# A three-stage graph pipeline on one core: one semaphore per step, packed float32 scores, a new order of work

## The chip, the cores and the metric

The kernel runs on one NeuronCore of a Trainium2 chip. A core has a matrix engine (TensorE, PE in the rows), a vector engine (VectorE, DVE), a scalar engine for activation functions (ScalarE, ACT), GpSimd (POOL) and SyncE (SP), which here only issues DMAs. Each engine runs its own list of instructions strictly in order, and the engines meet through semaphores: an instruction waits until a counter has reached a value, and raises another when it is done. The metric is the time of one execution on the device in microseconds, as the median of several.

## What is computed

Sixteen graphs of 512 nodes with 256 features each go through four layers, each on the layer-normed and rectified state, each added to the state:

```python
h = relu(layernorm(x)); x = x + L0(h, adj)   # hypergraph convolution twice, layer norm between them, plus h
h = relu(layernorm(x)); x = x + L1(h, adj)   # attention "transition" matrix, two hops
h = relu(layernorm(x)); x = x + L2(h, adj)   # 8 heads of 32 features
h = relu(layernorm(x)); x = x + L3(h, adj)   # relu((adj @ h) @ K) * mask

# L1: e = leaky_relu(sj[j] + si[i] + ab);  alpha = A * exp(e);  T = alpha / rowsum(alpha)
#     H = X W0 + T X W1 + T T X W2 + biases, then relu
# L2: Xp = X Wp (per head), Xc = Xp C^T;  attn = tanh(A * (Xc Xp^T));  out = relu(attn Xp)
```

## The kernel before

One graph is four tiles of 128 nodes (NT = 4) by 256 features. The work is a software pipeline over graphs. Every engine has a list of steps that it goes through once for each turn; a step is written with a delay, and in turn b it works on graph b minus that delay. Steps whose names begin with `f_` are the front, layers L0 and L1; steps whose names begin with `k_` are the back, layers L2 and L3. In each turn PE does the front of one graph and the back of the graph before it, so that the matmuls of the back fall where the front waits for a hand-off. The loop body is written out once and run by a hardware loop; the first and last turns are unrolled. A graph's back ends one turn after its front, so the last graph's back runs alone.

The front, in order, with the matmuls of each step: `f_m` and `f_u` (incidence transposed times h, incidence times that), `f_conv1` (times W1), `f_zT` (transposes of the normed hidden state z), `f_xw` (times W2), `f_m2`, `f_y` (incidence products again), `f_hT` (transposes of L1's input h1), `f_sj` and `f_q` (products of h1 with weights), then the softmax-like part on ACT and DVE (`f_exp`: two exponentials for each of four row tiles; `f_alpha`: their maximum and the product with adj; `f_sums`, `f_trans`: the division), `f_tt` (transposes of the transition matrix), `f_r` and `f_x2` (the two hops). Nearly every product is made in split float32: each operand is a high part and a low part of type fp32r, and three products (`three`) stand in for one. For this each PSUM tile is read twice: ACT copies it out as the high part, and DVE then subtracts that copy from the PSUM tile and writes the low part. Such a pair is called a hand-off below. PSUM holds three one-bank tiles `ring_f` for the front, two two-bank tiles `ring_b` for the back, and one bank `pv_acc` in which the attention output is summed.

The back: `k_norm2`, `k_hT`, `k_xp`, `k_xc` (projections of all heads), then eight attention units `k_unit` 0 to 7. A unit is four heads by one tile of 128 rows: PE makes the scores of four heads (`k_scores`), DVE multiplies them by the adjacency tile (the gate, L972, two halves of 1024 columns), ACT takes tanh (L579, two halves), and PE multiplies the result with Xp (`k_attend`, L1292, four matmuls into four strips of 32 columns). Then `k_outT`, layer norm 3 (`k_stats3`, `k_norm3`), `k_ax` (adjacency times h, plain float32) and `k_out`.

The scores are made by stacking: three 32-row groups (high, high, low of one operand against high, low, high of the other) are put on 96 partitions of `stk_p` and `stk_c`, by 24 DMAs a graph issued on SP (L331), after DVE and POOL have made the high and low parts (L952, L447, L956). One fp32r matmul of 96 rows then does a head's scores. `ring_b` has two halves, and the scores of a unit's second half can start as soon as DVE has read that half.

DMA loads are issued on SP in the order x, adjT (`rows`), the weight row (`wrow`), adj, adjT again for the back (`at`), and the store. `next_x` waits for `xh_sum` (POOL has read the x before), `next_adjt` for the transposes of `f_tt`. POOL computes the reciprocal roots of the layer norms with a power (L409, L413).

Every engine has one or two counting semaphores for most of its outputs (`drained`, `hi_made`, `full`, `full_b`), which are raised in the order of the code. A step that is moved therefore changes the counts of all.

## Time and profile before

| what | value |
|---|---|
| runs of the kernel before | 1858.55 us median of 3 (1858.37 to 1859.98) |
| profiled execution: device time, span | 1858.6 us, 1856.8 us |
| PE busy | 1544.6 us, 83% |
| DVE busy | 1193.9 us, 64% |
| ACT busy | 892.4 us, 48% |
| POOL busy | 273.9 us, 15% |
| mean granted TensorE clock | 0.92 |

The profiled execution's time is 1.8 us above its span, and 0.05 us above the median. A row of the timeline gives start, duration, engine, line, operation, output and inputs, shapes, and in brackets how long the engine was idle before it and who released it. Matmuls are pipelined: the next group starts before the duration of the last one has run out, so lengths of PE work are read as differences of starts. A float32 matmul appears as two records.

### The profile page before, as it was taken

How to read it: one execution, taken by the hardware profiler on the slowest of the kernel's cores; microseconds unless marked ns; L12 is line 12 of the kernel's file. 1: busy time of each engine (PE TensorE's matmuls, PEld its weight loads, DVE VectorE, ACT ScalarE, POOL GpSimd, SP SyncE). 2: the span in 40 equal slices, each digit the busy share in tenths (PEclk: the TensorE clock that was granted, in tenths of full speed). 3: DMA queues.
4: the chain of work that ended last, by engine and by line, in shares of the span. 5: the costliest groups of instructions: out<-in, count | busy, mean ns of one | idle time of the engine just before them, and what ended most of it. 6: DMA issues, size and time to landing. Idle time of an engine off the chain costs nothing.

```text
span 1856.8 us, 26984 instructions
## 1 busy us (share of the span) xinstructions
PE 1544.6 (83%) x9334; PEld 1195.9 (64%) x9334; DVE 1193.9 (64%) x2650; ACT 892.4 (48%) x1479; POOL 273.9 (15%) x167
## 2 busy tenths in 40 slices
PE   5587988989889888988989898897989889888855
PEld 4576675757667576776757677675767667666632
DVE  5565758677575866757585675758667575765523
ACT  2335546454454645445454534645454464545433
POOL 1101120111202011120201112020111201112010
PEclk8788998989899898989989898998989999898978
DMA  5013132132313213231321323123031412313030
GB/s 157 12 52 79 52 99 67 35 80 74 90 51 93 71 34 79 73 90 51 82 82 34 79 73 90 51 69 94 23 90 57 107 51 58 85 44 80 22 81 11
DMA packets 80806, 125.51 MB, mean 68 GB/s; under 512 B 10177, under 2 KB 29185, under 8 KB 80769
## 3 DMA queue, kind: packets, MB, share of 16 engines
q1 hardware_dynamic: 80768, 125.02, 24.1%
q8 instruction: 23, 0.38, 0.1%
q14 instruction: 15, 0.11, 0.0%
HBM read 66.27 MB, written 8.39 MB: 40 GB/s over the span
## 4 chain that ended last, share of the span: by engine, by line
PE 51%; DVE 16%; issue 16%; ACT 10%; POOL 6%; SPq 1%; DMA 0%; DVEq 0%; POOLq 0%; ACTq 0%
PE ring_f L1026 29%; PE ring_b L1026 15%; DVE att L972 7%; ACT hf L488 3%; PE ring_f L1182 2%; POOL xp_s L447 2%; POOL xf L430 2%; POOL xf L428 2%; ACT att L601 1%; PE ring_f L1212 1%; DVE rows L904 1%; PE ring_f L1124 1%; PE pv_acc L1292 1%; DVE rows L885 1%; POOL rstd_f L409 1%
## 5 line engine op out<-in xcount | busy, mean ns | idle before, releaser
L1026 PE MATMUL ring_f<-m,inc_n 128*128 128x256 f32 x2048 | 324.6, 289 | 16.7 <-POOL m L420 14.1
L972 DVE TENSOR_TENSOR att<-ring_b,at 128x1024 f32<-128x1024 f32 x256 | 299.2, 1216 | 35.7 <-PE ring_b L1026 33.8
L579 ACT ACTIVATE att<-att 128x1024 f32<-128x1024 f32 x256 | 263.6, 1066 | 100.3 <-DVE att L972 94.3
L1026 PEld LDWEIGHTS ring_f<-m,inc_n 128*128 128x128 f32 x2048 | 289.8, 194 | 25.1 <-issue 20.8
L1026 PE MATMUL ring_b<-stk_c,stk_p 96*128 96x512 f32 x512 | 186.8, 483 | 61.5 <-DMA stk_c<-xc_s 44.5
L1026 PE MATMUL ring_f<-m,inc_t 128*128 128x256 f32 x1024 | 210.3, 284 | 14.5 <-DVE m L742 14.5
L1026 PE MATMUL ring_f<-w,uz 128*128 128x256 f32 (+1 forms) x896 | 188.9, 334 | 13.1 <-DVE uz L735 8.5
L1026 PEld LDWEIGHTS ring_b<-stk_c,stk_p 96*128 96x128 f32 x512 | 100.2, 223 | 148.0 <-issue 71.4
L409 POOL TENSOR_TENSOR rstd_f<-var_f,mhalf 128x4 f32<-128x4 f32 x48 | 48.5, 1010 | 922.2 <-DVE var_f L726 922.2
L1026 PEld LDWEIGHTS ring_f<-w,uz 128*128 128x128 f32 x896 | 152.3, 192 | 34.2 <-DVE uz L735 14.9
L1026 PEld LDWEIGHTS ring_f<-m,inc_t 128*128 128x128 f32 x1024 | 160.3, 191 | 17.7 <-DVE m L742 17.7
L1292 PE MATMUL pv_acc<-att,xp_n 128*32 128x512 f32 x1024 | 134.2, 607 | 30.9 <-ACT att L579 29.9
L481 ACT ACTIVATE m<-ring_f,be 128x256 fp32r<-128x256 f32 x128 | 53.7, 470 | 170.9 <-PE ring_f L1026 169.0
L1026 PE MATMUL ring_b<-at,hb 128*128 128x512 f32 x256 | 117.8, 605 | 7.4 <-ACT hb L589 7.4
L474 ACT ACTIVATE uz<-ring_f 128x512 fp32r<-128x512 f32 x128 | 73.2, 598 | 100.2 <-PE ring_f L1124 43.0
L742 DVE SCALAR_TENSOR_TENSOR m<-ring_f,be,m 128x256 fp32r<-128x256 f32 x128 | 56.0, 479 | 83.0 <-ACT m L481 81.7
L1026 PE MATMUL ring_b<-xc_s,wp 128*128 128x512 f32 x192 | 72.9, 553 | 42.1 <-ACT att L601 38.8
L1026 PE MATMUL ring_f<-wk,uz 128*128 128x256 f32 x768 | 104.5, 285 | 0.0
L735 DVE TENSOR_TENSOR m<-ring_f,uz 128x512 fp32r<-128x512 f32 x64 | 41.4, 686 | 95.6 <-ACT uz L474 95.6
L1026 PEld LDWEIGHTS ring_f<-wk,uz 128*128 128x128 f32 x768 | 97.4, 191 | 2.8 <-DVE inc_t L735 2.7
L735 DVE TENSOR_TENSOR m<-ring_f,m 128x512 fp32r<-128x512 f32 x64 | 43.9, 687 | 85.7 <-ACT m L474 85.7
L488 ACT ACTIVATE hf<-xf,off_f,rstd_f 128x256 f32<-128x256 f32 x64 | 33.2, 589 | 136.8 <-DVE off_f L730 136.8
(158 smaller groups left out, 2623.7 us busy)
## 6 DMA issues: line engine op xcount, KB each, us to landing
stk_p<-xp_s SPq DMA_DIRECT2D x192, 128.0 KB, 2.4
stk_c<-xc_s SPq DMA_DIRECT2D x192, 128.0 KB, 2.3
rows<-in_adjT SPq DMA_DIRECT2D x16, 1024.0 KB, 5.3
adj_n<-in_adj SPq DMA_DIRECT2D x16, 1024.0 KB, 8.5
at<-in_adjT SPq DMA_DIRECT2D x16, 1024.0 KB, 5.3
x_in<-in_x SPq DMA_DIRECT2D x16, 512.0 KB, 3.5
out_x<-xb SPq DMA_DIRECT2D x16, 512.0 KB, 2.9
wrow<-in_adj SPq DMA_DIRECT2D x16, 256.0 KB, 6.0
```

The costliest lines, as they stand in the source:

```text
L409: pool.tensor_tensor(rstd_f[:, k], var_f[:, k], mhalf[:], ALU.pow).then_inc(rstd_made.sem, 1)
L428: pool.tensor_tensor(xf[:], x_in[:], hf[:], ALU.add).then_inc(xh_sum.sem, 1)
L430: pool.tensor_tensor(xf[:], xf[:], b2_bc[:].unsqueeze(1).broadcast_to([P, NT, D]), ALU.add).then_inc(xh_sum.sem, 1)
L474: act.activation(dst, ring_f[tile % 3][:], ACT.Copy).then_inc(hi_made.sem, 1)
L481: ins = act.activation(dst_of(t), ring_f[tile % 3][:, i * D:(i + 1) * D], ACT.Copy, scale=be[:, t:t + 1])
L488: ins = act.activation(dst[:, i], src[:, i], ACT.Relu, bias=off[:, i:i + 1], scale=scale[:, i:i + 1])
L579: act.activation(v, v, ACT.Tanh).then_inc(tanh_made.sem, 1)
L735: dve.tensor_tensor(dst, ring_f[tile % 3][:], hi_part.bitcast(F32), ALU.subtract)\
L742: ins = dve.scalar_tensor_tensor(dst_of(t), ring_f[tile % 3][:, i * D:(i + 1) * D], be[:, t:t + 1], hi_of(t).bitcast(F32), ALU.mult, ALU.s ...
L972: dve.tensor_tensor(att[:, u % 2, 2 * half:2 * half + 2], pair(tile)[:], at[:, t].unsqueeze(1).broadcast_to([P, 2, N]), ALU.mult)\
L1026: ins = pe.matmul(dst, lhsT, rhs, start=(first and n == 0), stop=(last and n == len(pairs) - 1), skip_group_check=True)
L1292: ins = pe.matmul(pv_acc[h * KH:(h + 1) * KH, :], xp_n[:, t, ch:ch + KH], att[:, u % 2, h], start=(t == 0), stop=(t == NT - 1), skip_group ...
```

## The change

- Every step has a semaphore of its own. The bank that a front tile uses comes from a table (`TILES`, `BANKS`).
- No stacking: `xp_t` and `xc_t` hold Xp and Xc as float32 with the four heads of a part on four groups of 32 partitions. The scores of a unit are four float32 matmuls with 32 rows each, one after another, into the four banks of `ring_b`. The 24 DMAs a graph, the high and low parts of Xp (DVE L952, POOL L447) and the low part of Xc (DVE L956) go. All four banks are written at once, so a unit's scores wait until both halves of the unit before it have been gated.
- L1's `si` comes from two more columns of `wq` (258 columns in `f_q`), with one small DVE addition for each row tile; the four DVE products of `f_si` (L868) go. `f_exp` for row tile i now waits for `f_q` i. The copy of the state `k_keep` (L941) goes: `f_x2` writes to `xa`, and `k_outT` writes `xb` from it.
- The high and low parts of the transposed transition matrix are in `tr_h` and `tr_l`, no longer in `inc_n` and `inc_t`.
- The turn is cut at another place (`f_m` is the first step of PE's list), and the steps are in another order on all engines. Attention units run from `f_zT` on: on PE scores 0 stands ahead of `f_xw`, scores 1 behind it. On SP the load of x stands behind that of adjT, the store and `wrow`.

The core of the diff (the steps' bodies mostly only change the names of their semaphores). The lists of steps at its end are the orders of a turn on SyncE, TensorE, ScalarE and VectorE, in this sequence; the number ahead of a step is its delay:

```diff
-            def stack(dst, src, part, group, loaded):
-
-                for h in range(4):
-                    sp.dma_start(
-                        dst[32 * group:32 * group + 32, h:HEADS:4, :].bitcast(F32),
-                        src[32 * h:32 * h + 32, part, :].rearrange("p (t n) -> p t n", t=2).bitcast(F32),
-                    ).then_inc(loaded.sem, 16)
...
             def k_scores(g, u):
                 part, t = divmod(u, NT)
                 if u == 0:
-                    pe.wait_ge(stk_p_loaded.sem, stk_p_loaded.after(g, STACK_LOADS))
-                    pe.wait_ge(stk_c_loaded.sem, stk_c_loaded.after(g, STACK_LOADS))
-                for half in range(2):
-                    ps = bank_b(g, B_S + 2 * u + half)
-                    for k in range(2):
-                        h = 4 * part + 2 * half + k
-                        ins = products(ps[:, k], [(stk_p[0:STACK, h, t * P:(t + 1) * P], stk_c[0:STACK, h])])
-                    ins.then_inc(full_b.sem, 1)
+                    pe.wait_ge(xc_made.sem, xc_made.after(g, 1))
+                    pe.wait_ge(xn_made.sem, xn_made.after(g, 1))
+                else:
+                    pe.wait_ge(gated.sem, gated.after(g, 2 * u))
+                for h in range(4):
+                    head = slice(h * KH, (h + 1) * KH)
+                    ins = pe.matmul(ring_b[h // 2][:, h % 2], xp_t[head, part, t * P:(t + 1) * P], xc_t[head, part],
+                                    start=True, stop=True, skip_group_check=True)
+                    if h % 2 == 1:
+                        ins.then_inc(scored.sem, 1)
...
              def f_exp(g, i):
-
                 if i == 0:
-                    act.wait_ge(si_made.sem, si_made.after(g, 2))
-                    act.wait_ge(full.sem, full.after(g, T_SJ + 1))
+                    act.wait_ge(sj_full.sem, sj_full.after(g, 1))
+                act.wait_ge(si_made.sem, si_made.after(g, i + 1))
...
             # SyncE, the order of a turn
-                    (-1, next_x), (-1, next_adjt), (-1, next_wrow), (-1, next_adj), (0, next_at), (1, store),
-                    (0, stack_p), (0, stack_c),
+                    (0, next_adjt), (3, store), (0, next_wrow), (0, next_x), (0, next_adj), (1, next_at),
...
             # TensorE, the order of a turn
-                    (0, f_u), (0, f_conv1), (1, k_hT), (2, k_out), (1, k_xp), (0, f_zT), (0, f_xw, 0), (0, f_xw, 1),
-                    (1, k_xc), (0, f_m2), (0, f_y), (1, k_scores, 0), (0, f_hT), (1, k_scores, 1), (0, f_sj),
-                    (0, f_q, 0), (1, k_attend, 0), (1, k_scores, 2), (1, k_attend, 1), (1, k_scores, 3),
-                    (1, k_attend, 2), (1, k_scores, 4), (0, f_q, 1), (0, f_q, 2), (1, k_attend, 3), (0, f_q, 3),
-                    (1, k_scores, 5), (1, k_attend, 4), (0, f_tt), (0, f_r, 0), (1, k_scores, 6), (1, k_attend, 5),
-                    (1, k_scores, 7), (0, f_r, 1), (1, k_attend, 6), (1, k_attend, 7), (1, k_outT), (0, f_x2, 0),
-                    (0, f_x2, 1), (1, k_ax, 0), (-1, f_m), (1, k_ax, 1),
+                    (0, f_m), (2, k_out), (0, f_u), (1, k_hT), (0, f_conv1), (1, k_xp), (1, k_xn), (1, k_xc),
+                    (0, f_zT), (1, k_scores, 0), (0, f_xw, 0), (0, f_xw, 1), (1, k_scores, 1), (0, f_m2),
+                    (1, k_attend, 0), (1, k_scores, 2), (0, f_y), (1, k_scores, 3), (1, k_attend, 1),
+                    (1, k_attend, 2), (1, k_scores, 4), (1, k_attend, 3), (0, f_hT), (1, k_scores, 5), (0, f_sj),
+                    (0, f_q, 0), (1, k_attend, 4), (0, f_q, 1), (1, k_scores, 6), (0, f_q, 2), (0, f_q, 3),
+                    (1, k_attend, 5), (1, k_scores, 7), (1, k_attend, 6), (0, f_tt), (0, f_r, 0), (1, k_attend, 7),
+                    (0, f_r, 1), (1, k_outT), (0, f_x2, 0), (0, f_x2, 1), (1, k_ax, 0), (1, k_ax, 1),
...
             # ScalarE, the order of a turn (after)
+                    (0, f_h0), (2, k_xh, 1), (1, f_r, 0), (1, f_r, 1), (2, k_h3), (2, k_ax), (0, f_m), (1, k_h2),
+                    (0, f_u), (1, k_hT), (2, k_out), (0, f_relu), (1, k_xp), (0, f_z), (1, k_xn), (1, k_xc),
+                    (0, f_zT), (0, f_xw, 0), (0, f_xw, 1), (1, k_unit, 0), (0, f_m2), (1, k_unit, 1),
+                    (1, k_unit, 2), (1, k_unit, 3), (0, f_h1), (0, f_hT), (1, k_xh, 0), (1, k_unit, 4),
+                    (0, f_q, 0), (0, f_q, 1), (0, f_exp, 0), (0, f_q, 2), (0, f_q, 3), (0, f_exp, 1),
+                    (0, f_exp, 2), (0, f_exp, 3), (1, k_unit, 5), (1, k_unit, 6), (0, f_tt), (1, k_unit, 7),
...
             # VectorE, the order of a turn (after)
+                    (0, f_stats0), (0, offset, 0), (0, f_HT), (0, f_h0), (1, f_r, 0), (1, f_r, 1), (2, k_outT),
+                    (2, k_stats3), (2, offset, 4), (0, f_H), (2, k_mask), (1, f_x2, 0), (0, f_dn), (1, f_x2, 1),
+                    (1, k_stats2), (2, k_ax), (0, f_m), (1, offset, 3), (0, f_u), (1, k_hT), (0, f_conv1),
+                    (0, offset, 1), (0, f_zT), (1, k_unit, 0), (0, f_xw, 0), (0, f_xw, 1), (1, k_unit, 1),
+                    (0, f_m2), (1, k_unit, 2), (0, f_y), (0, f_stats2), (1, k_unit, 3), (0, offset, 2),
+                    (1, k_unit, 4), (0, f_hT), (1, k_unit, 5), (0, f_q, 0), (0, f_q, 1), (1, k_unit, 6),
+                    (0, f_alpha, 0), (0, f_q, 2), (0, f_q, 3), (0, f_alpha, 1), (0, f_alpha, 2), (0, f_alpha, 3),
+                    (0, f_sums), (0, f_trans), (0, f_tt), (1, k_unit, 7),
```

What stands in a row on SP in the loop body, of the kernel before (a row is one DMA instruction, what it waits for in brackets; ISA rows are waits):

```order
L284 ISA [waits xh_sum]
L284 DMA x_in<-in_x 128x4x256
L374 ISA
L293 ISA [waits full]
L293 DMA rows<-in_adjT 128x4x512
L364 ISA
L290 DMA wrow<-in_adj 128x512 [waits drained]
L369 ISA
L287 DMA adj_n<-in_adj 128x4x512 [waits trans_made]
```

And of the changed kernel, the start of SP's loop body:

```order
L324 ISA [waits tt_full]
L324 DMA rows<-in_adjT 128x4x512
L394 REGISTER_ALU
L395 ISA [waits y_made]
L395 DMA out_x<-xb 128x4x256
L321 DMA wrow<-in_adj 128x512 [waits dn_read]
L362 ISA
L315 ISA [waits xh_sum]
L315 DMA x_in<-in_x 128x4x256
L318 DMA adj_n<-in_adj 128x4x512 [waits trans_made,dn_read,incn_made]
```

The load of x was the first of the turn, with a wait of its own. Now it stands behind the wait for the transposes of `f_tt` (`tt_full`), and behind the issues of adjT, of the store and of `wrow`.

ACT around the place where the next graph's first activation and the copy of the attention output stand (hf<-x_in is `f_h0` of the next graph, xh_t<-pv_acc the copy that PE's `k_outT` waits for, m<-ring_f the high parts of `f_r`, hb<-xb layer norm 3), before:

```order
L474 ACTIVATE m<-ring_f 128x512 [waits full]
L473 REGISTER_ALU
L474 ACTIVATE m<-ring_f 128x512 [waits full]
L606 REGISTER_ALU
L488 ACTIVATE hf<-x_in,off_f,rstd_f 128x256 [waits off_made]
L488 ACTIVATE hf<-x_in,off_f,rstd_f 128x256 x3
L573 ACTIVATE xh_t<-pv_acc 128x512 [waits pv_made]
L589 ACTIVATE hb,msum<-xb,off_b,rstd_b 128x256 [waits off_b_made]
```

And after:

```order
L469 ISA [waits off_made0]
L471 REGISTER_ALU [waits xh_sum]
L462 ACTIVATE hf<-x_in,off,rstd 128x256 [waits max_made]
L462 ACTIVATE hf<-x_in,off,rstd 128x256 x3
L594 ISA
L452 ACTIVATE xh_t<-pv_acc 128x512 [waits pv_made]
L452 ACTIVATE m<-ring_f 128x512 [waits r_full] x2
L598 REGISTER_ALU
L600 REGISTER_ALU [waits off_made4]
L602 ACTIVATE hb,msum<-xb,off,rstd 128x256 [waits mask_made]
```

`f_h0` now stands ahead of the high parts of `f_r`, and still ahead of the copy xh_t; both belong to the turn that is ending.

ACT in the softmax part, after the change (m<-ring_f is the high part of a `f_q` tile, the pairs rows<-ring_f and hf<-ring_f are the two exponentials of one row tile, att<-att is tanh of half a unit, here of units 5 and 6):

```order
L452 ACTIVATE m<-ring_f 128x256 [waits q_full] x2
L539 ACTIVATE rows<-ring_f,si 128x512 [waits si_made,sj_full]
L542 ACTIVATE hf<-ring_f,si 128x512
L452 ACTIVATE m<-ring_f 128x256 [waits q_full] x2
L539 ACTIVATE rows<-ring_f,si 128x512 [waits si_made]
L542 ACTIVATE hf<-ring_f,si 128x512
L539 ACTIVATE rows<-ring_f,si 128x512 [waits si_made]
L542 ACTIVATE hf<-ring_f,si 128x512 [waits max_made]
L539 ACTIVATE rows<-ring_f,si 128x512 [waits si_made]
L542 ACTIVATE hf<-ring_f,si 128x512 [waits max_made]
L586 REGISTER_ALU
L588 ACTIVATE att<-att 128x1024 [waits gated]
```

And PE at the same place (wq products are `f_q` 2 and 3; pv_acc<-att is `k_attend` 5 and 6, ring_b<-xc_t is `k_scores` 7, ident,rows is `f_tt`):

```order
L992 MATMUL ring_f<-wq,uz 128x258 [waits q_lo,h1_lo]
L992 MATMUL ring_f<-wq,uz 128x258 x5
L992 MATMUL ring_f<-wq,uz 128x258 [waits q_lo,h1_lo]
L992 MATMUL ring_f<-wq,uz 128x258 x5
L1267 MATMUL pv_acc<-att,xp_n 32x512 [waits tanh_made]
L1267 MATMUL pv_acc<-att,xp_n 32x512 x3
L1248 REGISTER_ALU
L1251 MATMUL ring_b<-xc_t,xp_t 128x512 [waits gated]
L1251 MATMUL ring_b<-xc_t,xp_t 128x512 x3
L1267 MATMUL pv_acc<-att,xp_n 32x512 [waits tanh_made]
L1267 MATMUL pv_acc<-att,xp_n 32x512 x3
```

Before, ACT had units 0 to 2 ahead of and between the exponentials and units 3 and 4 right behind them, and attends 0 to 4 between `f_sj` and `f_tt` on PE; now units 5 and 6 stand behind all exponentials on ACT, and attend 5 is the first thing that PE does after `f_q` 3.

## Rows read from the trace of the kernel before

**Rows 1.** The page, part 1: busy time and share of the span by engine.
```profile
PE 1544.6 (83%) x9334; PEld 1195.9 (64%) x9334; DVE 1193.9 (64%) x2650; ACT 892.4 (48%) x1479; POOL 273.9 (15%) x167
```

**Rows 2.** Windows: a turn, an idle stretch, the stretch behind it (PEclk is the granted clock).
```profile
900.00:1009.00 109.00, 94.56 (x582) 73.49 (x581) 73.29 (x164) 55.28 (x92) 17.00 (x10) 0.94 0.25 70
930.40:933.80 3.40, 1.03 (x9) 0.83 (x7) 3.15 (x8) 0.00 (x0) 0.00 (x0) 1.00 0.76 163
933.80:944.00 10.20, 8.08 (x22) 6.22 (x23) 8.42 (x22) 5.16 (x8) 1.02 (x1) 0.50 0.14 49
```

**Rows 3.** Timeline of PE, one turn: where its stages start, and one row of the next.
```profile
913.54 0.39 PE L1026 MATMUL ring_f<-rowb,sel 128*128 128x256 f32 x1
...
937.99 1.97 PE L1182 MATMUL ring_f<-ident,hf 128*128 128x128 f32 x8 [2.04 <-ACT hf L488]
...
960.18 1.52 PE L1212 MATMUL ring_f<-ident,rows 128*128 128x128 f32 x12 [1.32 <-DVE rows L904]
962.84 3.12 PE L1026 MATMUL ring_f<-wk,uz 128*128 128x256 f32 x24
...
978.60 1.07 PE L1313 MATMUL ring_b<-ident,xh_t 128*128 128x128 f32 x8 [1.41 <-ACT xh_t L573]
...
988.61 3.60 PE L1026 MATMUL ring_b<-at,hb 128*128 128x512 f32 x8
991.65 4.39 PE L1026 MATMUL ring_f<-m,inc_n 128*128 128x256 f32 x32
...
1003.66 0.73 PE L1026 MATMUL ring_f<-w,uz 128*128 128x512 f32 x2 [0.51 <-DVE uz L735]
...
1087.84 0.41 PE L1313 MATMUL ring_b<-ident,xh_t 128*128 128x128 f32 x2 [1.41 <-ACT xh_t L573]
```

**Rows 4.** Timeline of PE: a unit's scores at half clock, an attend and scores at full clock.
```profile
933.88 2.07 PE L1026 MATMUL ring_b<-stk_c,stk_p 96*128 96x512 f32 x4 [2.44 <-DMA stk_c<-xc_s]
...
944.82 1.06 PE L1292 MATMUL pv_acc<-att,xp_n 128*32 128x512 f32 x8
945.82 1.20 PE L1026 MATMUL ring_b<-stk_c,stk_p 96*128 96x512 f32 x4
```

**Rows 5.** The page, part 5: the gate and tanh, by 1024 columns.
```profile
L972 DVE TENSOR_TENSOR att<-ring_b,at 128x1024 f32<-128x1024 f32 x256 | 299.2, 1216 | 35.7 <-PE ring_b L1026 33.8
L579 ACT ACTIVATE att<-att 128x1024 f32<-128x1024 f32 x256 | 263.6, 1066 | 100.3 <-DVE att L972 94.3
```

**Rows 6.** Groups of instructions of ACT: one of the two exponentials of a row tile.
```profile
L530 ACT ACTIVATE hf<-ring_f,si 128x512 f32<-128x512 f32 x64 | 45.1, 705 | 0.0
```

**Rows 7.** Timeline of SP: the issues of adjT and adj, wrow's between them.
```profile
963.07 0.37 SPq L293 DMA_DIRECT2D rows<-in_adjT  x1
...
964.18 0.37 SPq L287 DMA_DIRECT2D adj_n<-in_adj  x1
```

**Rows 8.** The page, part 6: size and median time from issue to landing.
```profile
rows<-in_adjT SPq DMA_DIRECT2D x16, 1024.0 KB, 5.3
adj_n<-in_adj SPq DMA_DIRECT2D x16, 1024.0 KB, 8.5
...
x_in<-in_x SPq DMA_DIRECT2D x16, 512.0 KB, 3.5
```

**Rows 9.** Timeline: from layer norm 0's statistics (DVE) over POOL to ACT's copy of the attention output.
```profile
966.43 1.40 DVE L716 BATCH_NORM_STATS2 bns_f<-x_in 128x6 f32<-128x256 f32 x4
...
968.66 1.01 POOL L409 TENSOR_TENSOR rstd_f<-var_f,mhalf 128x4 f32<-128x4 f32 x1 [33.03 <-DVE var_f L726]
...
975.92 2.06 ACT L488 ACTIVATE hf<-x_in,off_f,rstd_f 128x256 f32<-128x256 f32 x4
977.88 0.58 ACT L573 ACTIVATE xh_t<-pv_acc 128x512 f32<-128x512 f32 x1
```

**Rows 10.** Timeline of PE in the last graph's back, alone: scores 0, attend 7.
```profile
1797.45 2.05 PE L1026 MATMUL ring_b<-stk_c,stk_p 96*128 96x512 f32 x4 [15.11 <-DMA stk_c<-xc_s]
...
1822.06 1.06 PE L1292 MATMUL pv_acc<-att,xp_n 128*32 128x512 f32 x8 [1.20 <-ACT att L579]
```

979 lines of the change are left out of this document (501 added, 478 removed).

## The prediction

> **What bounds the kernel now.** I read the page's busy shares first: PE is busy 83% of the span, no other engine over 64% [rows 1]. Then two equal rows of PE's timeline a turn apart: the transposes of `k_outT` start at 978.60 and at 1087.84, so a turn takes 109.2 us [rows 3]. In that turn PE is busy 94.6 us, DVE 73.3, ACT 55.3 [rows 2]. PE walks the front of one graph, which is one chain of matmuls and hand-offs, and puts pieces of the other graph's back into its waits. So a turn is PE's work plus the waits that no piece fills. And there is the clock: where PE is busy only 1.03 of 3.40 us, the grant is 0.50 in the 10.2 us behind it [rows 2]; that is 1.2 instead of 2.4 GHz. A unit's scores there last 2.07 us instead of 1.20 [rows 4].
>
> From the rows [rows 3] I cut the turn into stages (the next turn's rows are the same plus 109.2): `f_m` to `f_conv1` 12.0 (991.65 to 1003.66), to `f_xw` 19.1 (913.54 plus 109.2 less 1003.66), to `f_hT` 24.4, to `f_tt` 22.2, to `k_outT` 18.4, to `k_ax` 10.0, to `f_m` 3.0. Sum 109.1.
>
> **Parts with one answer.** The stacking DMAs lie on no steady path except one wait of 2.4 us ahead of scores 0 [rows 4]; they cost 15.1 us once, in the last back [rows 10]. DVE loses the four products of `f_si`, the copy `k_keep` and the parts of Xp and Xc; at 73.3 of 109.2 us [rows 2] it is not the bound, so that is worth nothing by itself. The separate semaphores add no instruction that computes. The second pair of tiles `tr_h`, `tr_l` lets `f_H` run early, but PE had no wait there.
>
> **The scores.** Four float32 matmuls of 32 rows replace four stacked ones. The nearest row is an attend, four float32 matmuls in four strips of columns, 8 records in 1.06 us [rows 4]: they run side by side. If row strips do that too, a unit's scores take 1.1 us where they took 1.20, nothing in the sum. If they don't, each takes what one float32 matmul takes: eight records of `k_ax`, four matmuls, lie between 988.61 and 991.65 plus half a microsecond of tail [rows 3], 0.8 to 0.9 each, a unit 3.4, 2.2 more than now. I take 1.1, for the attend is the same arithmetic. The Trainium skill (TensorE: Matmul & The Clock Gate, part 3, packing small matmuls) gives 3.07 times for four row tiles of 32 rows and 512 columns; no run here shows row tiles, and an estimate by it is 1.1 us a unit.
>
> What changes is the rhythm. All four banks are filled at once, so scores of unit u+1 wait for both gates of u: scores 1.1, gate 2 x 1.17 = 2.4 [rows 5], 3.6 us a unit at least, and 1.07 more until half of its tanh is done.
>
> **The new order, stage by stage.** A matmul of 256 columns costs PE 0.12 (24 in 3.12 with their tail [rows 3]), an fp32r one of 512 columns 0.23 (four in 1.20 with the tail [rows 4]); the counts are in the code. I walk each engine's list with these.
> - `f_m` to `f_conv1`: `f_m` 4.2, `k_out` 24 x 0.12 = 2.9, `f_u` 16 x 0.21 = 3.4, `k_hT` 0.8: 11.3 (`k_out` and `k_hT` come in, half of `k_ax` goes). Before 12.0.
> - to `f_xw`: `f_conv1` 24 x 0.23 = 5.6, `k_xp` 12 x 0.23 = 2.8; then PE waits 1.5 for ACT's copy of Xp, since `k_xn` now follows at once; `k_xn` and `k_xc` 2.6; z is ready some 7.8 behind `f_conv1` (output and relu 1.4, statistics to offset 3.4 as in [rows 9], four activations like [rows 6] 3.0), but ACT puts the copies of Xn and Xc (1.0 each) ahead of those of `f_zT`, and the fourth `f_zT` tile waits for the first to be drained: 2.1 of waiting; with scores 0, 18.5. Before 19.1.
> - to `f_hT`: `f_xw` 52 x 0.12 = 6.2 and scores 1 (1.1, a good cover) 7.4; `f_m2`, attend 0, scores 2: 5.9; then `f_y` 3.9, and DVE has 0.9 + 2.2 for y and statistics; but the gate of unit 3 (2.4) stands on DVE ahead of `offset` 2, while POOL needs only 1.0, and tanh of unit 3 stands on ACT ahead of `f_h1` (2.1). PE fills with scores 3, attends 1, 2, scores 4, attend 3 and still waits 2.8 and 1.2: 12.9. Sum 26.2, before 24.4.
> - to `f_tt`: DVE has 14 us of gates, q, alpha and division; before it had one more gate. `f_q` i now precedes `f_exp` i, so the first exponential starts some 3 us later behind `f_sj` than it could. 19.1, before 22.2, of which 2.6 were half clock. But PE has too little here: attend 5 needs tanh 5, which on ACT stands behind all eight exponentials (8 x 0.7 [rows 6]). PE waits some 7 us behind `f_q` 3, and by [rows 2] (1.03 busy of 3.40) its clock falls. Attend 5, scores 7, attend 6 then take 1.9, 1.9 and 1.8 instead of 3.1, some 2.4 us late for `f_tt`. 21.5.
> - to `k_outT`: this is the largest term. `k_outT` waits for ACT's copy xh_t, which stands behind `f_h0` of the next graph, on before as well: statistics to variance 2.15, POOL 1.0, offset 0.2, `f_h0` 2.06, copy 0.58 [rows 9], 6.3 us with the hand-overs. Before, x had been loaded long ago. Now x is issued behind adjT, the store and `wrow`, and adjT waits for `f_tt`'s last transposes. How late does x land? Before, adjT, wrow and adj, 2.25 MB, were issued from 963.07 on; adj, the last, issued at 964.18, landed 8.5 later [rows 7, 8], 9.6 after the first. adjT itself landed after its usual 5.3, though the others were behind it: the queue serves in order. The new row is adjT 1.0, store 0.5, wrow 0.25, x 0.5: also 2.25 MB, so x lands 9.6 after adjT's issue. At the least it is its issue, 1.7 later (0.55 each, [rows 7]), plus 3.5 [rows 8], 5.2. I take 9.6, since it rests on the same bytes in the same queue. `f_tt` to its end is 2.7 (960.18 to 962.84): 2.8 + 9.6 + 6.3 = 18.7 until `k_outT`. PE's own work is over after 2.7 + 5.8 (`f_r` 0, 48 x 0.12) + 1.0 + 2.95 = 12.45, so it waits 6.3 us. Stage 18.7, before 18.4 (which held two more scores and two more attends).
> - to `k_ax`: 10.0 as before, plus 2.3, for the 6.3 us of waiting takes the clock down, and I take half of the 10.2 us of [rows 2] at half clock, five, since denser work follows here, of which some 2.3 are lost: 12.3. Layer norm 3 is 9.3 behind `k_outT` and stays hidden.
> - to `f_m`: the whole of `k_ax`, 6.4, before 3.0.
>
> The Trainium skill (DMA: Bandwidth & Descriptors, queues, rings and completion order) says that on each DMA engine descriptors are consumed in ring order. The landings above agree: 5.3 for the first, 9.6 for the last. If each transfer had its own way, x would come after 5.2, and by that the turn would be 4.4 us shorter, which is the first rival.
>
> **Sum.** 11.3 + 18.5 + 26.2 + 21.5 + 18.7 + 12.3 + 6.4 = 114.9. In the stage to `f_hT` and behind, a wait of 2.8 us may or may not take the clock down; half of the 2.6 us that this costs before (`f_hT` and `f_sj`) would be 1.3, but part of it is covered: 0.6. I take 115.5, 6.3 more than 109.2.
>
> Sixteen turns: the first front alone gains 2 (no units between) and loses 6 (DVE's low parts of `f_r` stand behind the statistics of the late x): +4. Fourteen turns with 6.3: +88. The last front has no next x, so neither the wait nor its clock: 6.3 - 8 = -2. The last back alone: 15.1 of stacking go, and eight units at 3.7 instead of 25.7 / 8 = 3.2 (1797.45 to 1823.1 [rows 10]) give +6: -9. Sum +81; against the profiled execution, 1858.6 + 81 = 1940. The median of before is the same within 0.1.
>
> **Rivals.**
> 1. *x comes early enough, so not slower.* Mechanism: the store and `wrow` do not hold x up, it lands 5.2 us after adjT's issue. `k_outT` then waits 1.9, its clock stays up: 115.5 - 4.4 - 2.3 = 108.8. First turn 0, 14 x (-0.4) = -6, last front -2, last back -9: -17, 1842. It decides from a landing at about 6 us on, where the sum is nil. For it: the store goes the other way, out of the chip's memory on the core, and `wrow` is small. Against: [rows 7, 8]. 0.14.
> 2. *The units in the earlier waits fill more than I walk out*: the gate of unit 3 is covered (-2.3), the first exponential starts right behind `f_sj` (-3.0), and the clock stays up (-5.3): turn 104.9, 4 - 14 x 4.3 - 11 - 9 = -76: 1782. For it: PE's own work is under 94.6 us a turn [rows 2]. 0.08.
> 3. *All waits as walked, the clock stays up*: 110.2 a turn, 4 + 14 - 5 - 9 = +4: 1863. Against: some 7 us without matmuls, where 2.4 were enough [rows 2]. 0.08.
> 4. *Row strips run one after another*: 2.2 x 8 = 17.6 us a turn, of which some 14 on the path: 1858.6 + 81 + 16 x 14 = 2164. For it: no row of this trace shows row strips. 0.05.
>
> **Numbers.** The forecast, 1940, has 0.65; its own range, a turn from 112.5 to 119.5, is 1895 to 2000. The range for 8 in 10 takes in rivals 3 and 1: 1840 to 2005. Slower by over 0.2%, about what a measurement of this kernel can tell from no change: 0.65 + 0.05 + most of rival 3 = 0.75. Same: 0.03. Faster: 0.22, rivals 1 and 2.
>
> **What would show it.** In the new profile: the turn at 115.5; PE idle some 6 us ahead of the transposes of xh_t, released by ACT's copy; DVE idle ahead of `bns<-x_in`, released by the DMA of x_in, with a median landing near 8 (issue to landing) for x; PE idle some 7 us ahead of an attend behind the last wq product, released by ACT's tanh; clock 0.5 behind both; scores of four heads in 1.1 us with overlapping records. If DVE does not wait for x_in, my largest term is wrong. If the attend behind wq waits under 3 us, my walk of the softmax part is. If a unit's scores last over 3 us, rival 4 holds.

## The result and the profile after

The changed kernel takes 1965.5 us (median of 4 runs, 1963.1 to 1969.0), the kernel before 1859.0 (median of 4, 1858.4 to 1860.0): a ratio of 1.057, 95% interval 1.056 to 1.059. The profiled execution took 1963.1, 104.6 more than that of before, and its span is 104.5 longer. The forecast was 1940, the range 1840 to 2005, and slower had the chance of 0.75. Of the runs below one, of the kernel with tanh 5 moved, fell into a slow state (2261.7 us, the others of that kernel 1947 to 1951), and its median leaves that run out.

The page, part 1 (engine, busy us and share of the span, instructions), beside [rows 1]:

```profile
PE 1579.0 (81%) x9850; PEld 1144.1 (58%) x9850; DVE 1207.0 (62%) x2512; ACT 897.1 (46%) x1479; POOL 233.6 (12%) x151
```

No engine has become the bound. PE is busy 34 us longer, at a mean grant of 0.904 instead of 0.921, and idle 70 us longer. Windows by stage of one turn, with the same borders as in [rows 3]: `f_m`, `f_conv1`, `f_xw`, `f_hT`, `f_tt`, the second half of the transposes of xh_t (half of that step lies ahead of the wait), `k_ax`, the next `f_m` (stretch, its length, busy us of the engines, then PEclk, the granted clock):

```profile
core 0: us, PE busy (x) PEld busy (x) DVE busy (x) ACT busy (x) POOL busy (x), PEclk, DMA share, GB/s
1069.00:1080.50 11.50, 11.50 (x82) 10.65 (x81) 3.94 (x8) 5.98 (x11) 0.52 (x1) 1.00 0.26 91
1080.50:1100.30 19.80, 15.16 (x75) 10.28 (x74) 12.34 (x20) 13.07 (x21) 8.09 (x4) 1.00 0.00 0
1100.30:1126.70 26.40, 23.79 (x181) 16.05 (x181) 18.38 (x31) 12.86 (x18) 1.02 (x1) 0.95 0.00 0
1126.70:1147.80 21.10, 15.27 (x87) 7.14 (x87) 14.91 (x33) 13.40 (x21) 0.00 (x0) 0.82 0.00 0
1147.80:1166.50 18.70, 12.72 (x101) 11.10 (x101) 9.92 (x27) 7.06 (x12) 1.01 (x1) 0.96 0.53 182
1166.50:1178.50 12.00, 12.00 (x81) 12.00 (x82) 9.19 (x18) 3.20 (x10) 3.37 (x2) 0.78 0.00 0
1178.50:1185.00 6.50, 6.50 (x17) 2.88 (x16) 5.74 (x22) 0.00 (x0) 0.44 (x1) 1.00 0.00 0
```

The turn is 116.0 us, where 115.5 was forecast. Stage by stage, forecast and measured: 11.3 and 11.5, 18.5 and 19.8, 26.2 and 26.4, 21.5 and 21.1, 18.7 and 18.7, 12.3 and 12.0, 6.4 and 6.5. Only the second is off by more than 0.4.

The waits of PE, over the whole span (what waited, what released it: us in total, times, longest):

```profile
PE pv_acc L1267 <- ACT att L588: 90.2, 16, 5.9
PE ring_b L1276 <- ACT xh_t L452: 77.9, 14, 7.4
PE ring_b L1251 <- DVE att L942: 49.8, 22, 2.6
```

The first is attend 5 behind tanh 5, the second the transposes of xh_t behind ACT's copy. The third is scores that wait for a gate, in each turn scores 4 for the gate of unit 3 (2.61 us in the turn above). Here are the first two in the turn above (timeline of PE: start, us, engine, line, operation, idle time before it and what ended it):

```profile
1141.87 1.93 PE L1267 MATMUL pv_acc<-att,xp_n 128*32 128x512 f32 x8 [5.83 <-ACT att L588]
1143.73 2.09 PE L1251 MATMUL ring_b<-xc_t,xp_t 32*128 32x512 f32 x8
1145.75 1.94 PE L1267 MATMUL pv_acc<-att,xp_n 128*32 128x512 f32 x8
...
1166.34 1.12 PE L1276 MATMUL ring_b<-ident,xh_t 128*128 128x128 f32 x4 [5.38 <-ACT xh_t L452]
```

And windows of the two waits and of what stands behind each:

```profile
1136.20:1142.00 5.80, 0.13 (x4) 0.13 (x8) 5.80 (x16) 5.80 (x10) 0.00 (x0) 0.92 0.00 0
1142.00:1147.80 5.80, 5.80 (x25) 0.97 (x24) 2.44 (x8) 1.71 (x2) 0.00 (x0) 0.50 0.00 0
1160.90:1166.40 5.50, 0.12 (x2) 0.07 (x1) 4.18 (x18) 2.67 (x6) 1.01 (x1) 0.86 0.23 84
1166.50:1171.00 4.50, 4.50 (x22) 4.50 (x23) 4.43 (x10) 0.74 (x2) 0.00 (x0) 0.50 0.00 0
```

Behind each wait PE has no gap, and the grant is 0.50, 1.2 GHz. The chain that ends in the second wait starts on SP (timeline of SP, then of DVE, in the same turn):

```profile
1150.66 0.37 SPq L324 DMA_DIRECT2D rows<-in_adjT  x1
...
1152.52 0.51 SPq L315 DMA_DIRECT2D x_in<-in_x  x1
```

```profile
1160.10 1.08 DVE L734 BATCH_NORM_STATS2 bns<-x_in 128x6 f32<-128x256 f32 x3 [5.98 <-DMA x_in<-in_x]
```

x is there 9.4 us after adjT was issued, 7.6 after its own issue; [rows 8] had 3.5 for x. DVE stands idle for it, and ACT's `f_h0` and the copy of xh_t follow.

**The new scores.** Group of PE by line (busy us, mean ns of a record, idle before):

```profile
L1251 PE MATMUL ring_b<-xc_t,xp_t 32*128 32x512 f32 x1024 | 170.5, 739 | 50.9 <-DVE att L942 49.8 <-ACT xc_t L452 1.1
```

A unit is 8 records of 739 ns on average, and yet it lasts 1.14 us at full clock, where the stacked form of [rows 4] needed 1.20. The records overlap; the four strips of rows run side by side, as the run with one strip shows below.

**The row that was not forecast.** Timelines of POOL and of DVE in the stage to `f_xw`:

```profile
1089.02 1.02 POOL L415 TENSOR_TENSOR rstd<-var,mhalf 128x4 f32<-128x4 f32 x1 [3.51 <-DVE var L729]
1090.01 2.34 POOL L427 TENSOR_TENSOR xf<-x_in,hf 128x1024 f32<-128x1024 f32 x1
```

```profile
1090.07 2.30 DVE L739 SCALAR_TENSOR_TENSOR off<-sums,rstd 128x4 f32<-128x4 f32 x1 [1.13 <-POOL rstd L415]
```

The offset is a product of four columns, and lasts 0.16 us elsewhere [rows 9]. Here it lasts 2.30, and ends when POOL's sum ends. In the new order POOL has `f_sum` right behind rstd 1 and h0's low part right behind rstd 4; 30 of the 80 offsets last over 2 us. In the kernel before it is one, since POOL did the long ones elsewhere.

**Where the 104.5 us lie.** The first matmuls of `f_sj` cut the span the same way in both kernels. After, second and last graph but for the first two:

```profile
89.38 2.90 PE L992 MATMUL ring_f<-uz,v 128*128 128x512 f32 x6 [0.65 <-DVE uz L743]
...
194.72 1.64 PE L992 MATMUL ring_f<-uz,v 128*128 128x512 f32 x6
...
1828.41 1.66 PE L992 MATMUL ring_f<-uz,v 128*128 128x512 f32 x6
```

And before:

```profile
85.30 2.05 PE L1026 MATMUL ring_f<-uz,v 128*128 128x512 f32 x4 [0.69 <-DVE uz L735]
...
176.93 1.91 PE L1026 MATMUL ring_f<-uz,v 128*128 128x512 f32 x4
...
1706.08 2.33 PE L1026 MATMUL ring_f<-uz,v 128*128 128x512 f32 x5
```

Up to the first: +4.1. First to second: 105.3 against 91.6, +13.7. Fourteen turns to the last: 1633.7 against 1529.2, +104.5, that is 7.5 a turn (116.0 to 117.4 each, and one of 119.3). From there to the end of the span: 132.9 against 150.7, -17.8.

### The profile page after: what moved, and what is told of

Read it like the earlier page. It is cut to its first block, busy times and chain, and to the rows that moved or that the text cites. A ratio compares the mean times of both kernels' runs of the same rounds, so it can differ in the third digit from the quotient of the medians.

```text
span 1961.3 us, 26230 instructions
## 1 busy us (share of the span) xinstructions
PE 1579.0 (81%) x9850; PEld 1144.1 (58%) x9850; DVE 1207.0 (62%) x2512; ACT 897.1 (46%) x1479; POOL 233.6 (12%) x151
## 3 DMA queue, kind: packets, MB, share of 16 engines
q1 hardware_dynamic: 50048, 74.66, 11.4%
## 4 chain that ended last, share of the span: by engine, by line
issue 50%; PE 32%; POOL 6%; ACT 5%; DVE 5%; DMA 1%; SPq 0%; POOLq 0%; ACTq 0%; DVEq 0%
PE ring_f L992 18%; PE ring_b L992 8%; PE ring_b L1251 2%; POOL xb L434 2%; ACT hf L462 2%; POOL xf L429 1%; POOL xf L427 1%; DVE att L942 1%; POOL rstd L415 1%; ACT att L616 1%; PE pv_acc L1267 1%; DMA x_in<-in_x 1%; PE ring_b L1276 1%; PE ring_b L1212 1%; DVE bns L734 1%
## 5 line engine op out<-in xcount | busy, mean ns | idle before, releaser
L415 POOL TENSOR_TENSOR rstd<-var,mhalf 128x4 f32<-128x4 f32 x80 | 80.9, 1011 | 1493.9 <-DVE var L729 1493.9
L1251 PE MATMUL ring_b<-xc_t,xp_t 32*128 32x512 f32 x1024 | 170.5, 739 | 50.9 <-DVE att L942 49.8
L992 PE MATMUL ring_f<-m,tr_h 128*128 128x256 f32 x1024 | 187.8, 285 | 0.0
L992 PEld LDWEIGHTS ring_f<-m,tr_h 128*128 128x128 f32 x1024 | 159.5, 192 | 12.6 <-issue 12.6
L992 PE MATMUL ring_f<-m,inc_n 128*128 128x256 f32 x1024 | 136.6, 292 | 15.6 <-POOL m L419 14.9
L992 PEld LDWEIGHTS ring_f<-m,inc_n 128*128 128x128 f32 x1024 | 127.2, 194 | 33.8 <-issue 21.6
L992 PE MATMUL ring_f<-m,tr_l 128*128 128x256 f32 x512 | 145.0, 283 | 0.0
L452 ACT ACTIVATE m<-ring_f 128x512 fp32r<-128x512 f32 (+1 forms) x128 | 60.7, 486 | 160.3 <-PE ring_f L992 158.4
L743 DVE TENSOR_TENSOR m<-ring_f,m 128x512 fp32r<-128x512 f32 (+1 forms) x128 | 69.0, 551 | 73.7 <-ACT m L452 73.4
L739 DVE SCALAR_TENSOR_TENSOR off<-sums,rstd 128x4 f32<-128x4 f32 x80 | 77.6, 970 | 55.0 <-POOL rstd L415 55.0
```

The source lines that it names most:

```text
L415: pool.tensor_tensor(rstd[k][:], var[k][:], mhalf[:], ALU.pow).then_inc(rstd_made[k].sem, 1)
L452: act.activation(dst, src, ACT.Copy).then_inc(made.sem, 1)
L739: dve.scalar_tensor_tensor(off[k][:], sums[k][:, :, 0], -0.5, rstd[k][:], ALU.mult, ALU.mult)\
L743: dve.tensor_tensor(dst, src, hi.bitcast(F32), ALU.subtract).then_inc(made.sem, 1)
L992: ins = pe.matmul(dst, lhsT, rhs, start=(first and n == 0), stop=(last and n == len(pairs) - 1), skip_group_check=True)
L1251: ins = pe.matmul(ring_b[h // 2][:, h % 2], xp_t[head, part, t * P:(t + 1) * P], xc_t[head, part], start=True, stop=True, skip_group_check ...
```

## The experiments

Each kernel is the changed kernel with the edit shown, but for one that edits the kernel before. Times are medians; a ratio is against the kernel before in the same session.

### x issued first

```
-  (0, next_adjt), (3, store), (0, next_wrow), (0, next_x), (0, next_adj), (1, next_at),
+  (0, next_x), (0, next_adjt), (3, store), (0, next_wrow), (0, next_adj), (1, next_at),
```

> SP issues the next graph's x ahead of adjT, the store and wrow; nothing else moves. Theory (the landing of x behind adjT in SP's queue sets when f_h0 ends, and so when ACT copies xh_t): x lands long before DVE asks, the idle 5.4 us of PE ahead of the second half of the transposes of xh_t go, and with them the 2 us that x2's own part loses at half clock. Turn from 116.0 to about 108.6, total 1963 - 15 x 7.4 = 1852, between 1840 and 1870. Rival (the copy of xh_t is late because of what stands ahead of it on ACT and DVE, not because of x): DVE then waits for adjT instead, PE still waits 3 us or more, and the total stays above 1915.

Measured: 1884.4 us, ratio 1.012 (1.011 to 1.014), 81 less than the changed kernel; about 111 a turn. The landing of x, then PE's wait, then the held-up offset on DVE, then PE's scores 0 in the next turn:

```profile
DMA to landing us min/median/max: 3.3/3.5/3.6
```

```profile
1122.02 3.24 PE L992 MATMUL ring_b<-at,hb 128*128 128x512 f32 x7 [1.65 <-ACT hb L602]
```

```profile
1116.96 2.35 DVE L739 SCALAR_TENSOR_TENSOR off<-sums,rstd 128x4 f32<-128x4 f32 x1 [1.12 <-POOL rstd L415]
```

```profile
1159.28 2.09 PE L1251 MATMUL ring_b<-xc_t,xp_t 32*128 32x512 f32 x8
```

The wait ahead of the transposes is gone, as the theory says, and with it three quarters of the loss. Of the 111 us expected 30 did not come, for two reasons. `k_ax` now waits 1.65 us for layer norm 3. I had called that chain hidden. It is late by the held-up offset, 2.35 instead of 0.16, which the late x had covered. And from `f_m` to `f_hT`, where nothing was moved, the turn takes 60.4 us instead of 57.7: scores 0 runs at half clock there (2.09 instead of 1.14), and the step behind it is longer too.

The edit takes two things from x at once: the transfers ahead of it, and the wait for `f_tt`'s transposes that adjT has. x is now issued 59 us ahead of adjT (1041.41 and 1100.57).

### The copy of xh_t ahead of the next h0, on ACT

```
-  (0, f_h0), (2, k_xh, 1), (1, f_r, 0), (1, f_r, 1),
+  (2, k_xh, 1), (0, f_h0), (1, f_r, 0), (1, f_r, 1),
```

> On ACT the copy of the second half of xh_t (k_xh 1) stands ahead of f_h0 of the next graph; x is still loaded late. Theory: the transposes of xh_t no longer wait (5.4 to 0), so the late x reaches PE only through the low parts of r, which stand behind f_h0 on ACT and f_HT on DVE; PE waits about 3 us there, behind its own part of x2. About 3.3 us of that work has gone into the wait, and the clock falls for less: turn about 112, total about 1905. Rival (the late x costs the same wherever it is met): PE waits 5 us or more for the low parts of r, total within 10 us of 1963.

Measured: 1970.4 us, ratio 1.060 (1.058 to 1.063). Nothing gained; the rival's case. Timeline of PE:

```profile
1045.92 1.03 PE L1276 MATMUL ring_b<-ident,xh_t 128*128 128x128 f32 x8
...
1053.40 0.58 PE L992 MATMUL ring_f<-rowb,sel 128*128 128x256 f32 x1 [4.78 <-DVE m L743]
```

The transposes do not wait, but PE stops 4.8 us further on, in the middle of x2's own part, where I had counted that part as cover: its second half goes into the bank that held r's first half, and that bank comes free with the low part of r on DVE, which stands behind the late x's statistics too.

### Tanh 5 ahead of the copy of q 1, and both moves

```
-  (0, f_q, 0), (0, f_q, 1), (0, f_exp, 0), (0, f_q, 2), (0, f_q, 3), (0, f_exp, 1),
-  (0, f_exp, 2), (0, f_exp, 3), (1, k_unit, 5), (1, k_unit, 6),
+  (0, f_q, 0), (1, k_unit, 5), (0, f_q, 1), (0, f_exp, 0), (0, f_q, 2), (0, f_q, 3), (0, f_exp, 1),
+  (0, f_exp, 2), (0, f_exp, 3), (1, k_unit, 6),
```

> On ACT the tanh of unit 5 stands between the copies of q 0 and q 1 (where ACT is idle 1.5 us), no longer behind the eight exponentials. Theory: attend 5 and scores 7 no longer wait 5.8 us behind the wq products, attend 6 then runs at some 1142.4 on the scale of the turn that begins at 1068.97, and f_tt starts when DVE has divided the last rows, 2.5 us earlier than now. Turn 113.5, total about 1926. Rival (the softmax on DVE sets when f_tt starts, the idle time ahead of attend 5 costs nothing): turn 116, total within 5 us of 1963.

Measured: 1948.3 us (1947.1 to 1950.7), ratio 1.048 (1.045 to 1.050), 17 less, where 37 were expected. The steady turn is 116.1, as without the edit; the gain lies in the turns that were longer than that and in the early ones (115.9 a turn on average instead of 116.7). Timeline of PE, attend 6, `f_tt` and r's own part:

```profile
1134.23 1.06 PE L1267 MATMUL pv_acc<-att,xp_n 128*32 128x512 f32 x8 [3.84 <-ACT att L588]
1136.99 3.70 PE L1165 MATMUL ring_f<-ident,rows 128*128 128x128 f32 x16 [1.70 <-DVE rows L901]
1140.38 3.85 PE L992 MATMUL ring_f<-wk,uz 128*128 128x256 f32 x24
```

`f_tt` does start earlier, 8.7 us behind the last product of q instead of 11.6. But one wait of 5.8 has become two of 3.8 and 1.7, and the half clock falls on `f_tt` (3.70 for its sixteen, where 12 of them take 1.62 in the changed kernel) and on r's own part (3.85 instead of 3.14). More is lost further on: from `f_m` to `f_hT` the turn takes 60.0 us instead of 57.7, with scores 0 at 2.09, as with x issued first.

> Both moves together: x issued first on SP, tanh of unit 5 ahead of the copy of q 1 on ACT. Theory: the two waits lie in different stages and add up: turn 116.0 - 7.4 - 2.5 = 106.1, total about 1815, under the 1859 of the kernel before. Rival (one wait is the shadow of the other, since DVE or ACT sets the turn): the total is that of the better one of the two alone.

Measured: 1855.4 us, ratio 0.998 (0.997 to 1.000). The two moves together save 110, where they save 81 and 17 alone. So neither wait is the shadow of the other. 148 were expected, 38 more; alone the two moves had missed 30 and 20.

### All scores in one strip of rows

```
   for h in range(4):
+      head = slice(0, KH)
       ins = pe.matmul(ring_b[h // 2][:, h % 2], xp_t[head, part, t * P:(t + 1) * P], xc_t[head, part],
```

> All four scores of a unit read the first 32 rows of xp_t and xc_t, so all four lie in one strip of rows of the array; the output is that of head 0 four times, and not the reference's. Everything else is as in the changed kernel. Theory (four strips run side by side): a unit's scores go from 1.14 us to about 4 x 0.85 = 3.4, +2.3 for each of eight units; of these 18 us a turn some 10 to 14 lie on PE's path, the rest fills waits: total 2110 to 2170. Rival (four float32 matmuls of 32 rows are short anyway, whatever strip they lie in): 1.14 us, total 1965.

Measured: 2554.0 us, ratio 1.373 (1.371 to 1.376), 589 more than the changed kernel, some 37 a turn. Timeline of PE (scores 1), and windows of scores 0 and 1:

```profile
1099.47 3.69 PE L1252 MATMUL ring_b<-xc_t,xp_t 32*128 32x512 f32 x8
```

```profile
1084.60:1091.70 7.10, 7.10 (x10) 2.48 (x9) 1.98 (x3) 0.60 (x1) 0.00 (x0) 0.50 0.00 0
1099.50:1103.10 3.60, 3.60 (x10) 1.38 (x9) 2.60 (x3) 2.49 (x3) 0.00 (x0) 1.00 0.00 0
```

At full clock a unit takes 3.69 instead of 1.14: strips of rows are what makes the new scores cheap, and the price of 3.4 that I had worked out for the serial case was right within a tenth. What was not expected is the clock: in half of the units of the turn it falls to 0.50, and three of them take 7.2 us each. In the first of these PE is busy without a gap; in the 12.6 us ahead of it, it was busy 8.35, and the grant was 0.86. The mean grant of the run is 0.79, against 0.90. Eight times 2.55 us and the half clock of four units make 33 of the 37 us; that part of it would fill waits, as I had expected, was wrong.

### POOL's order

```
-  (0, p_rstd, 0), (2, p_rstd, 4), (0, f_h0), (1, p_rstd, 3), (2, k_y), (0, p_rstd, 1),
-  (0, f_sum), (0, p_rstd, 2),
+  (0, p_rstd, 0), (0, f_h0), (2, p_rstd, 4), (1, p_rstd, 3), (0, f_sum), (2, k_y),
+  (0, p_rstd, 1), (0, p_rstd, 2),
```

> Of the changed kernel only POOL's order is edited: h0's low part stands ahead of rstd 4, and the sum xf (f_sum) behind rstd 3, ahead of y; so no long POOL instruction starts right behind a rstd whose offset DVE is waiting to compute. In the trace of the changed kernel the offsets behind rstd 1 and rstd 4 last 2.3 us instead of 0.16, exactly beside POOL's 2.35 us of f_sum and f_h0. Theory (DVE's offset is held up by POOL's instruction): both go to 0.16; z is ready 2.1 us earlier, PE's waits ahead of the f_zT tiles (0.34 + 0.32 + 0.38 + 0.38 and 1.82) shrink by 2 us; offset 4 gains nothing yet, since the late x hides it. Turn 114, total about 1933. Rival (the 2.3 us are an artefact of the records, or f_sum ahead of y makes another wait): total within 5 us of 1963.

Measured: 1913.1 us, ratio 1.029 (1.028 to 1.031), 52 less than the changed kernel. DVE, and PE at `f_zT`:

```profile
1060.81 0.16 DVE L739 SCALAR_TENSOR_TENSOR off<-sums,rstd 128x4 f32<-128x4 f32 x1 [1.13 <-POOL rstd L415]
```

```profile
1063.60 1.59 PE L1075 MATMUL ring_f<-ident,rows 128*128 128x128 f32 x12
```

The offset is 0.16 again, and the four short waits in `f_zT`'s first tiles are gone; the stage is 2.1 us shorter. So the hold-up is real and is POOL's doing. The turn is 112.6, another 1.3 less. Little of that comes up to `f_hT` (0.2): attend 3 runs in 1.06 instead of 1.94, but PE then waits 0.90 for h1. The rest lies behind `f_hT`, where steps lose less to the half clock (`f_hT` itself 1.09 instead of 1.51, attend 6 1.57 instead of 1.94). The Trainium skill (SBUF — State Buffer, Who interferes with whom) says that a DVE instruction with two inputs in SBUF contends with a GpSimd instruction that reads SBUF, and that the one that starts second is blocked for the whole of the other. The trace agrees: 2.30 us beside 2.34.

### The three moves together

> x first on SP, tanh 5 ahead of the copy of q 1 on ACT, and POOL's order as in the run that edits it alone. Theory: with x early, offset 4 is on PE's path too: the wait of 1.65 us ahead of k_ax goes, and the half clock behind it (0.6), and 2 us ahead of f_zT as in the other run: turn 108.7 - 4.2 = 104.5, total 1855 - 15 x 4.2 = 1792, 3.6% below the kernel before. Rival (DVE or ACT now sets the turn): not under 1830.

Measured: 1785.0 us, ratio 0.960 (0.959 to 0.961), 7 from the 1792 expected. So the change with three places of its orders mended is 4% faster than the kernel before, and these three places held the whole loss. What of the 4% comes from the new scores, from the place of the units, from the products that went or from the moves themselves, no run here separates.

### x as late as in the change, but nothing else behind it

```
 ACT
-  (0, f_h0), (2, k_xh, 1), (1, f_r, 0), (1, f_r, 1), (2, k_h3), (2, k_ax),
+  (2, k_xh, 1), (1, f_r, 0), (1, f_r, 1), (2, k_h3), (0, f_h0), (2, k_ax),
 DVE
-  (0, f_stats0), (0, offset, 0), (0, f_HT), (0, f_h0), (1, f_r, 0), (1, f_r, 1), (2, k_outT),
-  (2, k_stats3), (2, offset, 4), (0, f_H),
+  (1, f_r, 0), (1, f_r, 1), (2, k_outT), (2, k_stats3), (0, f_stats0), (2, offset, 4), (0, offset, 0),
+  (0, f_HT), (0, f_h0), (0, f_H),
 POOL
-  (0, p_rstd, 0), (2, p_rstd, 4),
+  (2, p_rstd, 4), (0, p_rstd, 0),
```

> x is loaded as late as in the changed kernel, behind adjT, store and wrow. But everything of the two graphs in work that stood behind the layer norm of that x is put ahead of it: on ACT the copy of xh_t, r's copies and layer norm 3 ahead of f_h0; on DVE r's low parts, k_outT and the statistics of layer norm 3 ahead of those of x; on POOL rstd 4 ahead of rstd 0. Theory (a late x costs only what stands behind it in the order of ACT and DVE): the transposes of xh_t and x2 do not wait, h0 is ready some 5 us before f_m: turn 108.5, total about 1850, as good as or better than issuing x first. Rival (x's landing itself is too late for the next graph's front): PE waits ahead of f_m instead, total over 1920.

Measured: 1902.8 us, ratio 1.023 (1.021 to 1.024), 63 less than the changed kernel and 18 more than with x first; turn 112.6. The landing of x, then PE:

```profile
DMA to landing us min/median/max: 3.5/7.7/9.3
```

```profile
1032.86 4.62 PE L992 MATMUL ring_b<-k,ax_s 128*128 128x256 f32 x24 [2.51 <-DVE ax_s L743]
```

x is as late as ever, and no matmul waits for it, neither the transposes nor `k_ax` nor `f_m` (none of their rows has idle time before it). DVE does not wait for it either: x is issued at 1001.70, and DVE comes to its statistics at 1014.37, straight from those of layer norm 3. The lateness costs only what stands behind it. But the work that I put last is late now: the low part of ax on DVE stands behind `f_HT`, `f_h0`, `f_H` and `f_dn`, and `k_out` waits 2.5 us for it and runs at half clock (4.62 instead of 3.0). My 1850 left that out. Most of that wait, by these rows, is a second hold-up beside POOL, made by the edit itself. DVE has no gap from `f_H` to the low part of ax, and in it stands `k_mask`:

```profile
1022.91 2.32 DVE L964 TENSOR_SCALAR mask<-msum 128x4 f32<-128x4 f32 x1
```

It takes 0.17 in the changed kernel and 2.3 here (median of 16), and ends when POOL's low part of h0 ends (1021.94 to 1025.20). So this run shows that the late x need not be waited for, and not what such an order would give at best. The rival's wait ahead of `f_m` did not come.

### Matmuls in the wait ahead of attend 5

```
+  def warm(g, n, unit=None):
+      ...
+          pe.wait_ge(gated.sem, gated.after(g, 2 * unit + 2))
+          ps = ring_b[0][:, 0, 0:D]
+      for _ in range(n):
+          products(ps, [(h1_t[:, 0, 0:P], wq[:, 0, 0, 0:D])])
   def k_attend(g, u):
+      if u == 5:
+          warm(g, 36, 6)
```

> The changed kernel with 36 extra fp32r matmuls of 256 columns ahead of attend 5, into the bank that scores 7 overwrites, once unit 6 is gated; their results are not used. They fill 4.3 us of the 5.8 us in which PE waits for tanh 5. They test the term for the clock alone: nothing else is moved. Theory (attend 5, scores 7 and attend 6 run at half clock only because of that wait): the three take 1.07, 1.14 and 1.07 us instead of 1.93, 2.09 and 1.94, f_tt starts 2.6 us earlier; turn 113.4, total about 1925. Rival (what follows takes the gain back: f_tt waits for DVE's rows, or the wait ahead of xh_t grows by as much): total within 8 us of 1963.

Measured: 1944.2 us, ratio 1.045 (1.043 to 1.047), 21 less than the changed kernel, where 38 were expected. Timeline of PE:

```profile
1122.42 4.58 PE L992 MATMUL ring_b<-wq,uz 128*128 128x256 f32 x36 [0.81 <-DVE att L942]
1127.44 1.07 PE L1269 MATMUL pv_acc<-att,xp_n 128*32 128x512 f32 x8 [0.45 <-ACT att L588]
1128.44 1.14 PE L1251 MATMUL ring_b<-xc_t,xp_t 32*128 32x512 f32 x8
1129.51 1.06 PE L1269 MATMUL pv_acc<-att,xp_n 128*32 128x512 f32 x8
```

Attend 5 starts as late as before, and the three steps behind it take 3.1 us instead of 5.8: that they were slow was the clock alone, and the term of 2.4 in the forecast had the right size. In the turn that I read half of the gain, 1.4 us, is lost again up to `f_xw`, where nothing was moved:

```profile
1083.22 2.09 PE L1251 MATMUL ring_b<-xc_t,xp_t 32*128 32x512 f32 x8
```

Scores 0 took 1.14 there in the changed kernel. So the half clock also moves when a stretch of it is taken away. Over the fourteen turns the edit gives 1.8 us a turn (114.9 on average instead of 116.7), 25 us in all. Another part is lost once, at the end: from the last `f_sj` on it is 141.8 us instead of 132.9, for in the last back, alone, the 36 matmuls wait 2.5 us for the gate of unit 6 and then take 6.9, and attend 5 stands behind them.

### The best version, with matmuls in its waits

> The kernel with the three moves, and 28 such matmuls ahead of attend 6 and 11 ahead of f_tt (into f_tt's first bank, behind the low parts of q). Without them f_tt's transposes take 3.70 us instead of 2.3, and the 48 matmuls of r behind them 6.7 instead of 6.0, and scores 0 falls to half clock in some turns. Theory: the clock stays up through that stage, turn 104.8 - 1.7 = 103.1, total 1785 - 26 = 1759. Rival (the extra matmuls delay attend 6 or f_tt, or the clock falls elsewhere instead): 1780 to 1790, or more.

Measured: 1769.7 us, ratio 0.952 (0.950 to 0.954), 15 less than the three moves alone, where 26 were expected. PE's order is here as the next run has it; this run lacks the 18 ahead of scores 4.

```
+  (1, k_attend, 2), (0, warm, 18, HT), (1, k_scores, 4),
   ...
+  (1, k_attend, 5), (1, k_scores, 7), (0, warm, 28), (1, k_attend, 6), (0, warm, 11), (0, f_tt),
```

> The kernel with the three moves and the extra matmuls in two places, and 18 more of them ahead of scores 4, into f_hT's first bank, to fill the 2.6 us in which PE waits for the gate of unit 3. Without them attend 3 and f_hT run at half clock in most turns (1.93 and 1.75 instead of 1.07 and 1.09). Theory: f_hT is bound by the copy h1 and gains 0.7 us: turn 103.6 - 0.7 = 102.9, total 1770 - 10 = 1760. Rival (the clock falls elsewhere, or the extra matmuls overrun the gate): 1768 or more.

Measured: 1755.2 us, ratio 0.943 (0.941 to 0.944), the fastest; turn 102.3. The page of it:

```profile
PE 1583.8 (90%) x10762; PEld 1200.0 (68%) x10762; DVE 1145.5 (65%) x2512; ACT 895.9 (51%) x1479; POOL 235.7 (13%) x151
```

PE is as busy as in the changed kernel, with 912 more matmuls that compute nothing, in 208 us less; the mean grant is 0.977 instead of 0.904.

### The kernel before, with x issued last

```
-  (-1, next_x), (-1, next_adjt), (-1, next_wrow), (-1, next_adj), (0, next_at), (1, store),
+  (-1, next_adjt), (-1, next_wrow), (-1, next_adj), (-1, next_x), (0, next_at), (1, store),
```

> The kernel before, with one edit: on SP x is issued behind adjT, wrow and adj, no longer ahead of them. Theory (the queue serves in order, so x lands some 9.6 us behind adjT's issue, and what stands behind its statistics on DVE waits): in the trace of before adjT is issued at 963.07, so x lands at about 972.7, 6.3 us after its statistics start now (966.43); gates 6 and 7 stand behind them, and the rest of the turn moves by about as much: turn 109.2 + 6.2 = 115.4, total 1859 + 15 x 6.2 = 1952. Rival (this order of work hides the late x, as POOL's rstd and the gates wait for scores anyway): total under 1885.

Measured: 1967.6 us, ratio 1.058 (1.056 to 1.060). This one move in the kernel before costs as much as the whole change does. What DVE waits for, and the landing of x:

```profile
1032.07 1.41 DVE L716 BATCH_NORM_STATS2 bns_f<-x_in 128x6 f32<-128x256 f32 x4 [7.87 <-DMA x_in<-in_x]
```

```profile
DMA to landing us min/median/max: 3.6/9.6/11.1
```

x is issued 1.8 us behind adjT and lands 9.6 behind its own issue, so 11.4 behind adjT's. As in the changed kernel, the edit also puts x behind the wait that adjT has. I had taken 9.6 from adjT's issue, 1.8 us less: that is the side on which the run missed, by 16 us.

## Why the prediction was right, and where it was not

**The order of SP's queue.** This was the largest term, and it held in mechanism and size: x 9.6 us behind adjT forecast, 9.4 measured, the stage 18.7 and 18.7, PE's wait 6.3 forecast and 5.4 measured. By the run with x first it is worth 81 of the 107 us. That is the place in the queue as a whole: of the 6.0 us that DVE waits for x, 4.1 are the transfers ahead of it (7.6 less 3.5), and 1.9 would be left if x landed 3.5 behind its issue, for it is issued 1.9 behind adjT and so waits for `f_tt`'s transposes too. The first rival, x landing 5.2 behind adjT's issue, fell: what stands ahead of x does hold it up. How much of that is the store's, whose bytes go the other way, no run here separates. The landings speak for a good part: 2.25 MB with the store in them land in 9.4 us, 2.25 MB of loads in 9.6 [rows 7, 8], 2.75 MB of loads in 11.4.

**The clock behind the waits.** Two terms, 2.4 and 2.3 us. The steps behind attend 5's wait lost 2.7, and the run with matmuls in the wait shows that it was the clock. The stage to `k_ax`, with the other term in it, took 12.0 us where 12.3 were forecast. The third rival, that the clock stays up, fell. But the term is not additive: of 2.7 us given back in one place 1.8 a turn came out, and with x first or tanh 5 early scores 0 fell to half clock.

**The wait ahead of attend 5.** Some 7 us forecast, 5.8 measured, for the cause that was named, and tanh 5 moved took it away. `f_tt` was then 2.9 us earlier behind `f_q`, but the steady turn did not move; the clock took it.

**The gate of unit 3.** 2.8 forecast, 2.6 measured. The further wait of 1.2 ahead of `f_hT` was not there: attend 3 ran at half clock (1.94) and covered it. With attend 3 at 1.06, in the run with POOL's order, PE waits 0.90 there.

**The scores.** 1.1 us a unit forecast, 1.14 measured, and the run with one strip shows why. The fourth rival fell; its price, 3.4, was right at full clock.

**The step that failed in the turn** is the stage to `f_xw`: "statistics to offset 3.4 as in [rows 9]". The row was right for the place where it stood; in the new order POOL starts `f_sum` as soon as rstd 1 is out, and the offset takes 2.3 us. The prediction asked, of each moved step, what it waits for, but not what runs beside it. The stage came out 1.3 us too long; the other stages and the 0.6 for the clock, which was not needed, gave 0.8 back, and that the turn is right within 0.5 owes something to luck. By the run with POOL's order the hold-up is worth 2.1 us in the stage and 52 us in all, so the rest of the walk through that stage was 0.8 too long. (z at 5.6 + 7.8 = 13.4, waits of 2.1 and scores 0 make 16.6; the transposes of `f_zT`, some 2, are in the 18.5 and not in its text.) The same step hid in the sentence that layer norm 3 stays hidden: true only while x was late.

**The ends of the program.** The sum had +4 for the first turn, 14 x 6.3 = +88, -11 for the last front and back, +81 in all. Measured: up to the second `f_sj` +17.8, 14 turns +104.5, the rest -17.8. The turns gave 16 us of the miss of 23.5: the one that I read took 116.0, their mean is 116.7. The first turn gave 14 more; x2 waits 4.9 us for the low part of r there, which I had counted, and the cause of the rest stays open. The end gave 7 back, so these two misses hide one another in part. From the last `f_sj` to the transposes of xh_t it is 31.7 us against 36.6, to scores 0 34.2 against 54.7 (the stacking's 15.1 and 5.4 more), to the end of attend 7 35.3 against 25.7, and then 31.7 against 33.7. The eight units alone take 4.4 us each, where I had 3.7; and the +6 for them was a slip, since eight times 3.7 is 3.9 more than 25.7. The sum should have read +79, the forecast 1938. Measured they are 9.6 more:

```profile
1894.25 1.14 PE L1251 MATMUL ring_b<-xc_t,xp_t 32*128 32x512 f32 x8 [1.11 <-ACT xc_t L452]
...
1928.51 1.06 PE L1267 MATMUL pv_acc<-att,xp_n 128*32 128x512 f32 x8 [2.59 <-ACT att L588]
```

So the sign, the mechanism and the turn were right; the 23 us between 1940 and 1963 are sizes. The second rival, better filling, had a turn of 104.9. The three moves come to that (104.9 on average), and the extra matmuls 102.3, but not by its mechanism: the wait for the gate of unit 3 is as long as ever with the three moves (2.6), and it is the orders of SP, ACT and POOL that had to go with that of PE.

## What to carry to other kernels

Where a step is moved, look at three things besides its own wait: which transfers are now ahead of it in the queue that loads its input and what the first of them waits for (here a landing of 7.6 instead of 3.5 us behind an issue that waits for `f_tt`, together 81 of 107 us), what stands behind it on each engine that it passes (no engine waited for the late input any more once only its own graph's work stood behind it), and what a neighbour starts at the moment when its input comes free (2.3 us for a product of four columns beside POOL's sum). A change that looks slower may be a good one with three bad places: the waits, sorted by what released them, named two, a row that lasted 2.3 instead of 0.16 us the third, and each could be tried alone. And count half clock as a cost of the whole loop, not of the place where it shows: filling one wait with matmuls whose results are not used paid 1.8 of the 2.7 us that the rows there promised, filling three paid 30 us on the kernel with the three moves.

## What the hardware showed that I had not expected

- An offset of 128x4 on DVE, inputs in SBUF, takes 2.30 us instead of 0.16 while POOL adds two tensors of 128x1024 (2.34 us).
- Four float32 matmuls of 32 rows and 512 columns take 1.14 us in four strips of rows and 3.69 in one strip, a factor of 3.2.
- With all scores in one strip the grant was 0.50 through 7.1 us in which PE had no gap, and 0.79 over the whole run.
- A mask of 128x4 on DVE, with one input in SBUF, takes 2.3 us instead of 0.17 beside POOL's subtraction of 128x1024.
- Two short waits can cost as much clock as a long one: 3.8 and 1.7 us left `f_tt` at 3.70 us for its sixteen transposes.
